# The Mamba-2 mixer of a four-stage megakernel: the order of its batch products on TensorE and of taps, clamping and kernels on VectorE

## The reference, cut to what matters

```
proj = (rmsnorm(x) * norm_w) @ in_proj_w.T           # gate, hBC, dt
hBC  = silu(causal_conv(hBC, conv_w, conv_b))        # 4 taps;  hid, B, C = split(hBC)
A_cs = cumsum(-exp(A_log) * softplus(dt + dt_bias))  # per head, over time
M    = (C_i . B_j) * exp(A_cs_i - A_cs_j) for j <= i # one 256x256 kernel per head and batch
y    = M @ (hid * dt) + D * hid                      # what the chunked reference computes
out  = rmsnorm_by_group(y * silu(gate)) * gnorm_w @ out_proj_w.T
```

## Time and profile before

| | |
|---|---|
| median of 3 runs | 2665.6 us (2663.9 to 2677.38) |
| span of the profiled execution, first to last instruction | 2670.2 us; the profile gives no time of its own beside it |
| TensorE busy | 2308.2 us, 86% of the span |
| VectorE busy | 1957.9 us, 73% |
| ScalarE busy | 1460.8 us, 55% |
| GpSimd busy | 1238.2 us, 46% |
| granted TensorE clock, mean | 0.945 of full speed |

### The profile page before, as it was taken

One profiled execution on the slowest core, in us unless ns is written; L12 is line 12 of the kernel. 1 busy time (PEld: TensorE's weight loads), 2 busy tenths in 40 slices (PEclk: granted clock), 3 DMA queues, 4 the chain that ended last, 5 costly groups with the idle time before them and its releaser, 6 DMA issues. The chain is left out here.

```text
span 2670.2 us, 33973 instructions
## 1 busy us (share of the span) xinstructions
PE 2308.2 (86%) x11172; PEld 1672.4 (63%) x11172; DVE 1957.9 (73%) x3153; ACT 1460.8 (55%) x3092; POOL 1238.2 (46%) x788
## 2 busy tenths in 40 slices
PE   5966676667454999999999999999999999779997
PEld 4532222225434677777777777777777777569996
DVE  4559989994554786686685776775866866688777
ACT  2344444443103796685785866866956857742221
POOL 2119988993101464363462553644643624542212
PEclk9989998998576999999999999999999999899999
DMA  2030030000112232231332322322312312211010
GB/s 80 26 115 13 0 126 0 0 0 32 60 36 74 90 119 66 76 115 52 90 99 57 101 76 71 111 72 74 108 67 77 113 52 88 91 45 37 36 48 32
DMA packets 113218, 175.20 MB, mean 66 GB/s; under 512 B 9696, under 2 KB 77664, under 8 KB 112032
## 3 DMA queue, kind: packets, MB, share of 16 engines
q1 hardware_dynamic: 113056, 173.16, 20.6%
HBM read 166.71 MB, written 6.42 MB: 65 GB/s over the span
## 5 line engine op out<-in xcount | busy, mean ns | idle before, releaser
L78 PE MATMUL mg_pb<-xTh,mg_wh 128*128 128x512 f32 x1152 | 479.2, 416 | 16.9 <-POOL mg_wl L1233 16.9
L1243 POOL TENSOR_TENSOR mg_y<-mg_hT,mg_sg 128x512 f32<-128x512 f32 x128 | 187.7, 1466 | 598.9 <-DVE mg_hT L1479 598.9
L79 PE MATMUL mg_pb<-xTl,mg_wh 128*128 128x512 f32 x1152 | 454.3, 394 | 0.0
L80 PE MATMUL mg_pb<-xTh,mg_wl 128*128 128x512 f32 x1152 | 452.1, 392 | 0.0
L775 PE MATMUL ss_y<-ss_pr,cst 128*128 128x512 f32 x512 | 278.5, 678 | 125.7 <-POOL ss_pr L757 125.4
L1427 DVE SCALAR_TENSOR_TENSOR mg_hT<-mg_pb,mg_cw,mg_hT 128x510 f32<-128x510 f32 (+2 forms) x432 | 318.4, 741 | 31.6 <-ACT mg_hT L1599 22.8
L757 POOL TENSOR_TENSOR ss_pr<-o,ss_bc 128x1024 f32<-128x1024 f32 x128 | 301.9, 2374 | 45.9 <-DVE o L726 26.9
L1454 DVE TENSOR_TENSOR mg_m<-mg_gb,mg_cb 128x384 f32<-128x384 f32 x512 | 265.3, 549 | 71.6 <-ACT mg_gb L1649 68.2
L775 PEld LDWEIGHTS ss_y<-ss_pr,cst 128*128 128x128 f32 x512 | 98.4, 210 | 305.6 <-POOL ss_pr L757 225.8
L657 ACT ACTIVATE ss_da<-dt,ss_na 128x510 f32 (+1 forms) x256 | 165.9, 680 | 208.0 <-DVE o L726 208.0
L78 PEld LDWEIGHTS mg_pb<-xTh,mg_wh 128*128 128x128 f32 x1152 | 217.2, 189 | 76.5 <-issue 19.2
(11 more groups left out here) (289 smaller groups left out, 5217.4 us busy)
## 6 DMA issues: line engine op xcount, KB each, us to landing
mg_abc<-acs_rows SPq DMA_DIRECT2D x256, 256.0 KB, 3.4
mg_ws<-in_w_in SPq DMA_DIRECT2D x72, 512.0 KB, 3.8
ss_bc<-bc_rows SPq DMA_DIRECT2D x16, 1024.0 KB, 6.4
mg_wos<-in_w_out SPq DMA_DIRECT2D x64, 256.0 KB, 3.6
ff_ws<-in_w SPq DMA_DIRECT2D x7, 1024.0 KB, 4.7
x<-in_x SPq DMA_DIRECT2D x16, 256.0 KB, 4.1
ip_ws<-in_w_in SPq DMA_DIRECT2D x8, 512.0 KB, 3.6
ff_w2s<-in_w SPq DMA_DIRECT2D x7, 512.0 KB, 5.7
```

Source lines behind the costliest of these rows:

```text
L78: pe.matmul(out, lhs[0], rhs[0], start=start, stop=False)
L79: pe.matmul(out, lhs[0], rhs[1], start=False, stop=False)
L80: return pe.matmul(out, lhs[1], rhs[0], start=False, stop=stop)
L1243: pool.tensor_tensor(yb[:, p % RING, t], hT[s % 2][:, t], sg[s % 2][:, t], ALU.mult).then_inc(s_y2, 1)
```

## The change

Two lists are rewritten. On TensorE the products of batches 0 and 1 stand side by side: in steps with output tiles both come behind the first output tile (batch 0 later, batch 1 earlier), in the others behind the projection j = 2 (batch 0 later). On VectorE, in steps without output tiles, the clamping for batch 3 and the taps of j = 1 move ahead of kernels 4 and 5, so that kernels 4 to 7 stand in one row behind both projections' taps.

```diff
@@ TensorE, steps with a pair
                         turn(p, 1)
                         proj(s, 1, 0)
                         proj(s, 1, 1)
-                        y_mm(p, 0)
                         if outs:
                             out_tile(*outs[0])
+                            y_mm(p, 0)
+                            y_mm(p, 1)
                         proj(s, 2, 0)
                         proj(s, 2, 1)
-                        y_mm(p, 1)
+                        if not outs:
+                            y_mm(p, 0)
+                            y_mm(p, 1)
                         proj(s, 3, 0)
                         proj(s, 3, 1)
                         if outs:
@@ VectorE, steps without output tiles
                         kernel_of(p, 3)
                         times_step(p, 1)
                         taps(s, 0)
+                        clamp(p, 3)
+                        taps(s, 1)
                         kernel_of(p, 4)
                         kernel_of(p, 5)
-                        clamp(p, 3)
-                        taps(s, 1)
                         kernel_of(p, 6)
                         kernel_of(p, 7)
                         skip(p, 0)
```

## The result

The change makes the kernel 2% slower: 2728.94 us (median of 6 runs) against 2671.81 us (median of 6 runs of the kernel before, the three of the table above among them), a ratio of 1.0204 with a 95% interval of 1.0182 to 1.0226. That is 57.1 us; 55 were predicted, and 2728.94 lies inside the range of 2698 to 2745. Against the forecast of 2721 it is 8 us more, and 6.2 of these are the kernel before, whose six runs have a higher median than the three that the forecast started from.

What follows compares the result with a forecast made beforehand. TensorE was taken to bound steps with output tiles and r = 5, ScalarE to pace r = 6 to 8. Terms -2.8 + 43.4 + 8.4 + 5.6 = 54.6 us on 2665.6 gave 2721 us, range 2698 to 2745.

Steps and rivals of the forecast that it cites:

- r = 3 and 4, 14 steps: Steps with output tiles, bound by TensorE: products side by side save 0.3 us in each.
- r = 2, 7 steps: Steps with output tiles: the 0.3 us saving, less some 0.5 us of wait for VectorE's low parts in each.
- r = 5 to 8, seven groups: Steps with output weights: later kernel 4 delays ScalarE, making TensorE 6.2 us later per group, 43.4 us in all.
- r = 5 to 8, first group: Same steps with no output tiles ahead, so ScalarE isn't early: four steps at 2.1 us each, 8.4 us.
- r = 0 and 1: Steps inheriting ScalarE's 1.4 us of lag: between 0 and 1.4 us, taken as 0.7, 8 times, 5.6 us.
- r = 2 to 4, first group: Steps said to wait on other things; nothing was put on them.
- The pair: Two products in sequence on TensorE: 1.02 us for a single one, 0.70 for the second, so 0.3 us saved per step.
- The steps with output weights: Step lengths foretold for r = 5 to 8, with ScalarE's wait for VectorE's kernels growing to some 3 us per step.
- the rival that was priced at 14 us: GpSimd meets VectorE's clamping in each step: 0.43 us x 33 steps, 14 us more, 2735 us; chance 0.12.
- 2763: Rival: TensorE's clock falls after idling in 25 steps, 1.7 us each, 42 us more, 2763 us; chance 0.05.
- Absorption: Rival: ScalarE has the 2.1 us to spare, all 64 pairs save 0.3 us, 2646 us; chance 0.03 (half absorbed 0.04).
- half the wait: Rival: only half of ScalarE's 2.1 us stays in the 25 steps, 26 us less, 2695 us; chance 0.06.

Runs made afterwards that it cites:

- e2: Kernel before plus VectorE's part of the change alone, TensorE's order as before; 2733.68 us, ratio 1.0226 to the kernel before.
- e4: The change with only the taps of j = 1 ahead of kernel 4, clamping put back behind kernel 5; 2726.49 us, ratio 1.0197 to the kernel before.
- e3: The change with only the clamping ahead of kernel 4, taps of j = 1 put back behind kernel 5; 2696.09 us, ratio 1.0089 to the kernel before.
- e1: Kernel before plus TensorE's part of the change alone, VectorE's order as before; 2681.23 us, ratio 1.0028 to the kernel before.
- e6: Kernel before with GpSimd's addition to the sums of squares cut from 512 columns to 4; 2671.70 us, ratio 0.9996 to the kernel before.
- e7: The change, with VectorE instead of ScalarE clamping batch 1 in steps with output weights too; 2738.83 us, ratio 1.0241 to the kernel before.

## Why the prediction was right, and where its terms were off

Its main step held: `decay(p, 6)` waits for kernel 4, and seven instructions ahead of kernel 4 make the loop of ScalarE and VectorE longer. e2 shows that VectorE's order alone does it, e4 that the taps are the larger piece, the last group's r = 8 that GpSimd isn't needed for it. Term by term, the sum from the first turn to the last:

| term | predicted us | measured in the two traces |
|---|---|---|
| r = 3 and 4, 14 steps | -4.2 | -5.7 |
| r = 2, 7 steps | +1.4 | +1.7 |
| r = 5 to 8, seven groups | +43.4 | +43.2 (-3.2, +15.7, +15.7, +15.0) |
| r = 5 to 8, first group | +8.4 | +9.0 |
| r = 0 and 1 | +5.6 for 8 | +9.6 for 7 |
| r = 2 to 4, first group | 0 | -3.5 |
| sum | 54.6 | 54.3 |

That the sum is off by only 0.3 us is luck: three errors, -1.5, +4.0 and -3.5 us, cancel.

*The pair.* 0.3 us was taken, 0.41 came. The working priced the second product by the distance of the starts, 0.70; the pair's own row gives 1.68 us for both and so 0.36 saved. The last 0.05 is not resolved. The wait for the low parts in r = 2 came as stated: 26.94 us against 26.9.

*The steps with output weights.* 15.12 us for r = 5 (15.3 predicted), 17.81 for r = 6 (17 to 18.5), 18.41 for r = 7 and 8 (18.4); decay 6 waits 87.8 us in all (about 95).

*r = 0 and 1.* Mis-sized: 1.4 us each, where 0.7 was taken. Here the rival that was priced at 14 us came true in part. Timeline of VectorE and GpSimd in the r = 0 of the windows above:

```profile
1597.77 1.12 DVE L1473 TENSOR_SCALAR mg_nd<-mg_abc,mg_tabs 128x128 f32<-128x128 f32 x1
1598.81 0.27 DVE L1475 TENSOR_SCALAR mg_nd<-mg_abc,mg_tabs 128x128 f32<-128x128 f32 x1
...
1597.53 1.28 POOL L1260 TENSOR_TENSOR mg_ssq<-mg_ssq,mg_sq 128x512 f32<-128x512 f32 x1
```

The clamping meets the addition and loses 0.84 us, which kernel 4 inherits. It met GpSimd in before's r = 0 too (2.0 us for the four instructions, 1.7 in the change), but there behind kernel 5. Part of the 9.6 us is the clock, in the r = 0 of the sixth group. Windows of that step with r = 1, and of a stretch in it:

```profile
1974.69:2020.08 45.39, 43.66 (x217) 34.89 (x218) 30.70 (x52) 24.43 (x47) 22.14 (x16) 0.96 0.16 49
1991.46:1996.00 4.54, 4.54 (x18) 3.44 (x15) 4.47 (x6) 3.24 (x5) 4.18 (x4) 0.62 0.20 55
```

TensorE had waited 1.10 and 0.62 us just ahead for kernels 5 and 7; then a clock of 0.62, for the most part the lower level of 1.2 GHz, was granted over 4.54 us. The step takes 45.39 us, and 43.79 in the same place of e2, where the clock stayed at 1.00: 1.6 us. In the step shown above the same two waits, 1.08 and 0.62, were followed by a clock of 1.00.

*GpSimd and the clamping.* The prediction argued that the clamping would move away from GpSimd's work in r = 6 to 8. It did, but by little: the addition ends at 1562.31, the clamping starts at 1562.57. Its bound of 0.43 us was wrong. That was what one meeting cost in before; in e3 it was 1.07 us. The Trainium skill ("SBUF — State Buffer", section "SBUF: two separate sides") says that some VectorE instructions and those of GpSimd share a port pair, which the one that starts first holds for its whole instruction while the other is blocked. The traces agree: in before 33 of the 96 clampings took over 1 us, each of them began while an instruction of GpSimd ran, and none of the other 63 did.

*The first group.* Nothing was put on its r = 2 to 4, and 3.5 us came back. In before, clampings at the start of its r = 3 met several instructions in a row; timeline of VectorE, before:

```profile
895.12 1.08 DVE L1470 TENSOR_SCALAR mg_nd<-mg_abc,mg_tabs 128x128 f32<-128x128 f32 x1
...
897.32 2.37 DVE L1472 TENSOR_SCALAR mg_nd<-mg_abc,mg_tabs 128x128 f32<-128x128 f32 x1
899.61 0.68 DVE L1445 TENSOR_TENSOR mg_hc<-mg_tb,mg_tabs 128x512 f32<-128x512 f32 x1
```

That is what held the turn of the earlier trace rows: the time step stands behind four instructions that take 4.57 us. In the change the same four take 2.63 us, that turn waits 0.21 us in place of 2.71, and with the wait the low clock of the earlier trace rows is gone: the step's mean granted clock is 1.00, and the step takes 16.79 us in place of 20.00. Either part alone, e1 or e2, does the same, so it is a shift of meetings and not what the change was made for.

*The other rivals.* The clock stayed at 1.00 in all steps r = 5 to 8 of the change although TensorE idles 2.9 us in each r = 7 and 8, so 2763 is out; it fell in the one r = 0 above. In r = 6 to 8 of e4 it did fall now and then, and nothing came of it. Windows of e4, the start of a step r = 7 and then the whole step:

```profile
1547.44:1552.00 4.56, 4.56 (x17) 3.77 (x18) 1.26 (x2) 4.53 (x11) 4.38 (x4) 0.70 0.44 144
...
1547.44:1566.01 18.57, 16.72 (x89) 12.63 (x89) 14.41 (x25) 15.81 (x39) 11.48 (x9) 0.93 0.36 115
```

Ahead of it TensorE had idled 2.1 of 3.9 us. At 0.70 for 4.56 us, so for a part of them at the lower level of 1.2 GHz, the step takes 18.57 us, and 18.58 the next one at 1.00: TensorE spends its wait on it, as the prediction argued. Absorption and half the wait are out by the rows of r = 7 and 8.

*What lies outside.* The two spans differ by 59.7 us, 54.3 of it between the first and the last turn. Of the rest, 4.9 us lie ahead of the first turn (883.71 against 878.81), where the two programs are the same; over all profiles here that turn comes between 877.76 and 884.26 us. So they are no part of the change.

## What to carry to other kernels

When no engine is busy for a whole step, follow the loop of waits, and ask of each instruction whether it lies in it: 3 us moved ahead of one cheap instruction cost some 2.2 us in each of 25 steps, and the 0.4 us that TensorE won there only lengthened its wait. A piece of the change can be kept where its engine bounds the step (r = 3 and 4) and left out elsewhere. And an instruction that meets another engine's work has no fixed price: look for rows of one form whose duration varies (0.28 and 1.35 us here), find what ends with them, and move them to where the other engine stands idle before counting on any relief.

## What the runs showed of the hardware

VectorE's clampings and low weights, when they meet a running instruction of GpSimd, count as busy while they stand: 0.28 us became 1.35, 0.74 became 2.57. In the traces of all 14 kernels 730 clamping instructions took over 0.5 us, and each of them ended 0.08 to 0.09 us behind the recorded end of a GpSimd instruction. The taps, which read a PSUM bank, took 2.30 us beside a running GpSimd and beside an idle one. So VectorE's busy time of 13.9 us in r = 8 of before holds waiting that no view of waits shows. Shortening GpSimd's addition by 1.1 us (e6) gained nothing, as the next VectorE instruction met the next GpSimd one. Taking 1.17 us per step from an engine in the loop (e7) made nothing faster for the same reason, save in the last group's r = 8, where GpSimd was done early and it gave 1.18.
